# Selective scan: decayed state in a PSUM bank, one bank for the y products, copied out after pair 1

## The reference, cut to what matters

```
def step(h, inp):                       # h: (8 batches, 512 channels, 16 states)
    u_t, dt_t, B_t, C_t = inp
    dA = exp(clip(dt_t[..., None] * A, -20.0, 0.0))
    dB_u = clip(dt_t[..., None] * B_t[:, None, :] * u_t[..., None], -10.0, 10.0)
    h = clip(h * dA + dB_u, -100.0, 100.0)
    y = einsum('bds,bs->bd', h, C_t)
    return (h, y)
_, ys = jax.lax.scan(step, h0, xs)      # over 1024 tokens
```

## Time and profile before

| what | value |
|---|---|
| median of 3 runs | 6645.08 us (6643.51 to 6648.44) |
| profiled execution | 6640.38 us |
| its span, first to last instruction | 6638.7 us |
| scan, first `decayed` to last | 4413.3 to 5977.2 us |
| DVE busy in 4413 to 5984 us | 1427.13 of 1571 us |
| ACT, PE, POOL busy there | 1192.48, 1047.48, 625.55 us |

### The profile page before, as it was taken

One profiled execution on the slowest core, in us unless ns is written; L12 is line 12 of the kernel. 1 busy time (PEld: TensorE's weight loads), 2 busy tenths in 40 slices (PEclk: granted clock), 3 DMA queues, 4 the chain that ended last, 5 costly groups with the idle time before them and its releaser, 6 DMA issues. The chain is left out here.

```text
span 6638.7 us, 95330 instructions
## 1 busy us (share of the span) xinstructions
PE 5016.2 (76%) x27420; PEld 2058.7 (31%) x27420; DVE 4896.9 (74%) x9319; ACT 3869.7 (58%) x6353; POOL 1429.3 (22%) x1658
## 2 busy tenths in 40 slices
PE   6979799797979799795999644426666666667778
PEld 3333333333333333333666322201111111114555
DVE  6666564756666564755888688979999999996768
ACT  5555555555555555553444466667777777774443
POOL 0000000000000000000111244444433434434421
PEclk8989899898989999897999866655555555558999
DMA  0000000000000000001111233331111111114432
GB/s 23 1 13 1 14 1 1 14 1 14 1 14 1 14 1 1 7 1 36 41 41 43 64 116 115 113 97 43 42 44 44 42 43 42 44 40 151 154 98 70
DMA packets 198908, 273.62 MB, mean 41 GB/s; under 512 B 13989, under 2 KB 157989, under 8 KB 192454
## 3 DMA queue, kind: packets, MB, share of 16 engines
q1 hardware_dynamic: 181190, 252.90, 12.6%
q10 hardware_dynamic: 17408, 16.78, 0.7%
HBM read 151.14 MB, written 118.49 MB: 41 GB/s over the span
## 5 line engine op out<-in xcount | busy, mean ns | idle before, releaser
L643 DVE TENSOR_REDUCE at_nmax<-at_ps_s 128x1 f32<-128x1024 f32 x1024 | 1248.9, 1224 | 640.7 <-PE at_ps_s L342 639.4
L485 ACT ACTIVATE at_probsT<-at_ps_t 128x512 f32<-128x512 f32 x2048 | 1111.5, 594 | 831.5 <-PE at_ps_t L367 831.4
L1928 PE MATMUL sc_da<-sc_parts,sc_sel 24*128 24x512 bf16 x1024 | 527.0, 616 | 596.8 <-DVE sc_decayed L2017 507.1
L2027 DVE CUSTOM_DVE_ANT_0 sc_state<-sc_xd,sc_decayed 128x256 f32<-128x256 f32 x2048 | 787.6, 426 | 137.8 <-POOL sc_xd L1902 137.8
L1902 POOL TENSOR_SCALAR sc_xd<-sc_xd 128x1024 f32<-128x1024 f32 x512 | 584.4, 1141 | 942.5 <-ACT sc_xd L1987 942.5
L1981 ACT ACTIVATE sc_da<-sc_da,sc_a_col 128x1024 f32<-128x1024 f32 x512 | 557.1, 1088 | 375.4 <-PE sc_da L1928 375.3
L2017 DVE SCALAR_TENSOR_TENSOR sc_decayed<-sc_da,sc_state 128x256 f32<-128x256 f32 x2048 | 766.3, 416 | 6.4 <-ACT sc_da L1981 6.4
L363 PE MATMUL at_ps_t<-at_qkT 108*128 108x512 bf16 x2048 | 663.9, 385 | 64.9 <-ACT at_probsT L485 35.5
L342 PE MATMUL at_ps_s<-at_qkT 108*128 108x512 bf16 x2048 | 666.5, 410 | 26.3 <-DVE at_nmax L643 12.1
L1987 ACT ACTIVATE sc_xd<-sc_ps_du,sc_bt 128x512 f32<-128x512 f32 x1024 | 644.4, 684 | 0.0
L376 PE MATMUL at_ps_o<-at_probsT,at_v 128*32 128x256 f32 x8192 | 628.3, 390 | 1.4 <-ACT at_probsT L485 1.4
(11 more groups left out here) (307 smaller groups left out, 8059.1 us busy)
## 6 DMA issues: line engine op xcount, KB each, us to landing
dt_parts<-si_pt SPq DMA_DIRECT2D x64, 384.0 KB, 2.6
du_parts<-si_pu SPq DMA_DIRECT2D x64, 384.0 KB, 3.2
sc_parts<-dt_parts SPq DMA_DIRECT2D x128, 192.0 KB
sc_parts<-du_parts SPq DMA_DIRECT2D x128, 192.0 KB
u_tok<-si_ut SPq DMA_DIRECT2D x8, 2048.0 KB, 8.3
y<-sc_yo SPq DMA_DIRECT2D x256, 64.0 KB
so_yin<-y SPq DMA_DIRECT2D x32, 512.0 KB
so_uin<-u_tok SPq DMA_DIRECT2D x32, 512.0 KB
```

The lines of the kernel that those rows point to most:

```text
L485: nc.scalar.activation(probsT[:, c % RING, u * HALF:(u + 1) * HALF], ps_t[u][:], ACT.Exp).then_inc(s_exp, 1)
L643: nc.vector.tensor_reduce(nmax[:, par, t:t + 1], ps_s[t % 2][:], AX_X, ALU.max, negate=True).then_inc(s_max, 1)
L1928: dt_done = nc.tensor.matmul(da[q % 2][:, j], sel[0:KR, :], parts[0:KR, h, q % HP * 2 + j], start=True, stop=True)
L2027: nc.vector._custom_dve(bass.dve_ops.TENSOR_ADD_SAT, out=state[:, j % SRING, ch], in0=xd[:, q % RING, j % 2, ch], in1=decayed[:, ch], s0=S ...
```

## The change

Three things change together. `decayed` moves from SBUF to a PSUM bank of its own. To free that bank, the y products of all turns share one bank `ps_y`. So that one bank can serve, the y products are added one pair later (at q = 2, 4 and 6, and the last round of a turn at q = 0 of the next one), each turn's first y product waits until the bank of the turn before is copied (`s_yo >= it`), and the copy on ACT moves from behind pair 3 to behind pair 1. Banks in use stay at eight.

```diff
-        decayed = sb("decayed", [ROWS, DI])
...
-        ps_y = [psum(f"ps_y{g}", [P, HALF]) for g in range(2)]
+        ps_y = psum("ps_y", [P, HALF])
+        decayed = psum("decayed", [ROWS, DI])
...
                 if r == 0:
                     pe.wait_ge(s_cw, it + 1)
-                    if not (isinstance(it, int) and it < 2):
-                        pe.wait_ge(s_yo, it - 1)
+                    pe.wait_ge(s_yo, it)
...
-                    last = nc.tensor.matmul(ps_y[g][s * VW:(s + 1) * VW, :], cw[g][:, c0:c0 + VW],
+                    last = nc.tensor.matmul(ps_y[s * VW:(s + 1) * VW, :], cw[g][:, c0:c0 + VW],
...
-                    if q % 2 == 1:
-                        add_y(it, g, q // 2)
+                    if q % 2 == 0 and q > 0:
+                        add_y(it, g, q // 2 - 1)
+                    elif q == 0 and not first:
+                        add_y(it - 1, 1 - g, ROUNDS - 1)
...
             schedule(pe, turn)
+            add_y(NI - 1, 1, ROUNDS - 1)
...
-                nc.scalar.copy(yo[:, g], ps_y[g][:]).then_inc(s_yo, 1)
+                nc.scalar.copy(yo[:, g], ps_y[:]).then_inc(s_yo, 1)
...
-                    if q == HP - 1 and not first:
+                    if q == 1 and not first:
                         store(it - 1, 1 - g)
```

## The result

| kernel | median us | ratio to before, 95% interval |
|---|---|---|
| before | 6645.44 | |
| changed | 6776.86 (6772.53 to 6778.04) | 1.0196, 1.0178 to 1.0214 |

The change makes the kernel 131 us slower. The profiled execution took 6776.41 us. The first and last `decayed` are now at 4418.5 and 6109.3 us: the scan went from 1564 to 1691 us, 127 us more. Of the 136 us between the two profiled executions, the other 9 lie ahead of the scan (5) and behind it (4), where the code is the same. The clock is as before, half of full speed in the scan.

What follows compares the result with a forecast made beforehand. A loop through PE, ACT, POOL and DVE, 6.05 us per two pairs, was taken to bound the scan. 6640.4 + 156 (copy stall) - 14 - 20 (contention) = 6762 us, with 4.7 for the median 6767; range 6730 to 6830.

Steps and rivals of the forecast that it cites:

- The bound: In the scan, a loop through PE, ACT, POOL and DVE takes 6.05 us per two pairs; DVE only nearly bounds.
- The signs named beforehand: In the profile after: ACT idle 2.9 us before the copy, DVE 2.7 in two parts, copies 26.3 us apart.
- Part 1: ACT's copy waits for the y product, delaying pair 2's exp by 2.47 us a turn: 63 x 2.47 = +156 us.
- Part 2: decayed leaving SBUF ends contention between DVE's state and POOL: -14 us for the weights, -20 us for the clips.
- the rival in which the contention stays: In the scan, POOL waits for something else of DVE, so nothing is saved: 6801 us, chance 0.1.
- Part 3: DVE writing and reading PSUM in the scan: between +82 and -37 us at the ends, taken as 0.
- The +82 us end: Upper end for DVE's PSUM accesses in the scan: +0.08 us an instruction, x 4 x 256; dearer PSUM had chance 0.2.
- Part 4: In the scan, later y products, the first one's wait for the copy and the moved last one cost nothing.
- Sum: Whole kernel: 6640.4 + 156 - 14 - 20 = 6762 us profiled, 6767 as median; a turn about 26.3 us.

Runs made afterwards that it cites:

- E8: E5 with the y products of rounds 1 to 3 on 64 of the 512 channels only (y incomplete); 6455.33 us, ratio 0.9717.
- E10: Changed kernel with the y product of each turn's last round on 64 of the 512 channels only; 6681.12 us, ratio 1.0055.
- E5: E1 with POOL's clip split into two instructions, one for each step; 6570.76 us, ratio 0.9881.
- E9: E1, clip unsplit, with the y products of rounds 1 to 3 on 64 of the 512 channels only; 6611.46 us, ratio 0.9945.
- E1: Changed kernel with one edit: ACT's copy of y stands behind pair 2 instead of pair 1; 6609.57 us, ratio 0.9947.
- E3: Changed kernel with decayed back in SBUF and the copy behind pair 2; 6645.40 us, ratio 1.0001.
- E2: Changed kernel with decayed back in SBUF, all else as changed; 6973.10 us, ratio 1.0493.
- E7: Changed kernel with the y products where they were before (copy still behind pair 1) and POOL's clip split in two; 6571.27 us, ratio 0.9884.

## Why the prediction was right

**The bound (a loop over two pairs, not DVE).** Right. The loop is 5.97 us without contention, and DVE alone 5.3 (E8). It is shown by E10, where each us off the copy's wait came off the time, by E5, where a shorter clip brought the pairs closer together, and by E9, where 7/8 of three y products taken away changed nothing. The signs named beforehand are there: ACT idles 2.86 us in front of the copy (2.9 forecast), DVE 1.25 + 1.54 = 2.79 us in two parts (2.7), a turn takes 26.4 us (26.3), and two pairs behind the stall 5.97, not under 5.9.

**Part 1, the copy before the exp of pair 2.** Right in place, slightly small. It costs 8.54 - 5.97 = 2.57 us a turn, not 2.47, so 63 x 2.57 = 162 against 156 us, and E1 puts it at 167 (161 by the scans alone, 1690.8 us against 1530.1). The y product ends where I had it, 3.05 us after D(0). The 0.10 lies mainly in the handing over: the copy starts 0.15 us after the y product's modelled end (5002.96 + 1.94 = 5004.90, to 5005.05), where I had taken 0.04, from the decay matmuls; the exp then follows the copy's start by 0.48, not 0.51.

**Part 2, contention.** Right for this kernel: the weights take 405 ns, not 643, the clips 1.04 us throughout, and E1 against E3 gives 36 us where I had 34. The sum needed only what the contention cost in the kernel before, where I had read it. What I had not seen is that this price is good for that order alone. For the rival in which the contention stays I wrote 6801; E2, where it does, took 6973. The step "the contention costs 0.22 a turn and 0.08 per two pairs" is no property of the two instructions but of their phase. Counted in the changed kernel's order, PSUM saves 196 us.

**Part 3, PSUM for DVE.** I took 0. `decayed`, which now writes PSUM, takes 423 ns against 415 (409 in E2), and `state`, which now reads it there, 411 against 418 (410 in E2); starts of groups are 0.66 to 0.67 us apart as before. The +82 us end came from two ACT rows that differ in function and type too, and was far off. The Trainium skill's fixed costs ("VectorE: DVE Perf Modes", "The TRN2 errata"), 120 cycles with a PSUM source against 58, do not show in this two-input instruction: with one input moved to PSUM its median is 411 ns, and with both in SBUF 410 to 418.

**Part 4.** Right: E3, which has the single bank and the later y products, is at 1.0001.

**Sum.** 63 x 2.57 - 34 = +128 us, and the scan grew by 127. The forecast of +121 was low by 6 us of stall. The 3 us from there to the measured +131 lie outside the scan, where nothing changed and no cause is shown: over the twelve profiled kernels the scan starts anywhere from 4411.1 to 4423.3 us.

## What to carry to other kernels

When an instruction is moved ahead on an in-order engine, look up what its operand waits for on the engine that makes it, after that engine's own order has changed too: each of the two moves here was free alone, and together they made a wait of 2.9 us in a loop without slack. The slack of the busiest engine (0.35 us a pair on DVE) says nothing of whether a stall comes back; add up the loop link by link. And a contention measured in one schedule gives no price for another: the same SBUF operand cost 36 us in one order and 196 in the other.

## What the runs showed of the hardware

- With `state` reading two inputs from SBUF, a clip of POOL that starts in its first half shuts out the second half for the clip's whole 1.04 us; `decayed`, with one SBUF input and an SBUF output, is never held (425 ns at most, and E2).
- Moving the output of `decayed` to PSUM made it 8 to 14 ns longer (256 wide, float32; 423 against 415 before and 409 in E2), and the distance between starts did not grow.
- The handing over from PE to ACT was 0.15 us behind the float32 y product and 0.04 behind the bf16 matmuls, by modelled ends.
- Of the kernels that compute the whole result, E5 and E7 are the fastest, 6570.76 and 6571.27 us, 1.2% under the kernel before.
